# A four-layer vision block on one core: roots of the last layer norm in two chains instead of three, and half of a mask multiplication moved behind the transposes

## The chip, the cores and the metric

The kernel runs on one core of a Trainium2 chip. The metric is the device time of one execution in microseconds. The engines are PE (TensorE, matrix products and transposes), DVE (VectorE), ACT (ScalarE), POOL (GpSimd) and SP (SyncE, which here only issues DMAs). They run their own instruction streams and wait for each other through semaphores.

## The reference

The input is x, 128 x 128 positions with 32 channels. Four layers follow, each added to its input:

```python
x = x + L0_conv(ln_c(x), mask0, ...)
t = t + L0_ffn(ln_t(t), W, V, gamma, beta)       # a recurrence with a sigmoid
x = x + L1_conv(ln_c(x), mask1, ...)
t = t + L1_ffn(ln_t(t), router_w, router_b, expert_w, expert_b)   # 2 of 8 experts per token

def L1_conv(z, mask, ...):
    zn = layer_norm(z)
    a = mask * sigmoid(zn @ w_ag + b_ag) * (zn @ w_ap + b_ap)
    b = mask * sigmoid(zn @ w_bg + b_bg) * (zn @ w_bp + b_bp)
    p = einsum('bikc,bjkc->bijc', a, b)          # for each channel a 128x128x128 product
    return (layer_norm(p) @ w_z + b_z) * sigmoid(zn @ w_g + b_g)
```

The change concerns the third layer (its masks) and the layer norm ahead of the fourth (its roots).

## The kernel before

The 128 rows lie on the 128 partitions. Each partition holds 128 tokens of 32 channels. Work is cut into 8 groups of 16 tokens (GROUPS), and sums for the layer norms into 4 quarters of 32 tokens (QUARTERS). Nothing plans the order at run time: each engine's instructions are written out in one list, and an engine executes them strictly in that order. "Waits" below are waits on a semaphore at the head of such a list.

**Layer norms.** A `Norm` object has pieces, ranges of tokens for which the roots are taken together. For each quarter DVE makes the sums (`take_sum`, L331) and the sums of squares (`take_squares`, L369) of squares that ACT (`take_square`, L337) or POOL (L346) has made. `take_var` then runs a chain of eleven small DVE instructions (L375 to L398), each waiting for the one before; the last raises `done`. The length of an instruction of the chain hardly depends on how many tokens the piece has.

**Third layer, input stage.** `n_c` has pieces of 32, 32 and 64 tokens. For each group POOL (`scale_c`, L361, two instructions) multiplies by the roots (DVE does it for groups 0 and 1), PE transposes (`turn_group`, L651), ACT copies to SBUF (`copy_c`, L1607), PE makes the logits of the output gate (L1326) and, in two halves, the projections (L1338, biases by L1158). PE's order is that of `groups_held`: head 0, head 1, tail 0, head 2, tail 1, head 3, tail 2, tail 3, head 4, head 5, tail 4, and so on, a head being the transposes and a tail the projections. ACT takes the sigmoids (`gates_c`, L1613 and L1620), DVE multiplies both (`gate_c`, L1941) into `gated`, which is laid out [token i, channel, token j] with 64 channels (32 of a, then 32 of b). PE's half h of tail g waits until DVE has done the gate of the same half of group g - 1, which frees the PSUM banks. POOL multiplies `gated` by the mask, two instructions per group (`mask_half`, L833, all 64 channels). `mask_e` is the mask in the order of `gated`, built from `mask_c` before the stage. PE has twelve idle products (L1133) after the last tail and then waits for all sixteen masks.

**Third layer, products.** For q = 0 to 7, PE transposes 4 channels of a into bank q % 2 (L1362) and 4 of b into bank 2 + q % 2 (L1364). ACT copies the first to `gated_t` (L1638), DVE the second (L1972), PE multiplies them (L1353), ACT keeps the product (L1627) and squares it (L1633), DVE makes the partial sums (L1963, L1968). POOL has the bias of the gated output meanwhile (L941, L946). After it, DVE takes the roots, multiplies PE's projections by the gates (L1994) and POOL adds them to `x2` (L872).

**Fourth layer, input stage.** `n_d` has pieces of 32, 32 and 64 tokens. DVE takes the roots of quarter 0 as soon as its squares are summed, those of quarter 1 after its own, and those of quarters 2 and 3 together. POOL's `scale_d` waits for the roots of a piece and then scales its groups (L626, one instruction each). PE transposes them (L651) and makes the router's logits (L1417), ACT copies the transposed groups (`copy_d`, L1660). ACT's list is: squares of quarters 0, 1 and 2, `copy_d` of groups 0 and 1, square of quarter 3, `copy_d` of groups 2 and 3, and so on. From group 1's copy on, SP issues DMAs that repeat the transposed x in `out_gate` and, from group 3's copy on, in `x` (`copy_x`, L731). DVE chooses the two experts of each token in quarters 0 and 1 (`choose`, L2040 to L2066); after that PE spreads the weights (L1447), DVE weighs x by them (L2074), PE multiplies with the experts (L1468), ACT keeps the sum (L1697) and PE turns it back (L1479), group by group.

Of the kernel before, what the change touches and what calls it, by code (L numbers as in the profile page):

```python
# [35 lines left out]
P = 128  # L36
C = 32
# [37 lines left out]
def build(nc, a, out):  # L75
    ctx = ExitStack()
    with ctx:
        def sb(name, shape, dt=F32):
            return ctx.enter_context(nc.sbuf_tensor(name, shape, dt))

        def sem(name):
            return ctx.enter_context(nc.semaphore(name))
# [49 lines left out]
        mid128 = sb("mid128", [P, P])  # L132
        x2 = sb("x2", [P, P, C])
        mask_e = sb("mask_e", [P, P])
        ident_b = sb("ident_b", [P, P], BF16)
        pick = sb("pick", [P, S, 2, P], BF16)
        eighth = sb("eighth", [P, 16])
# [80 lines left out]
        a_copied = sem("a_copied")  # L218
        rows_built = sem("rows_built")
        w_scaled = sem("w_scaled")  # L220
        w_repeated = sem("w_repeated")
        w_kept = sem("w_kept")
        o_built = sem("o_built")
# [128 lines left out]
        def scale_c(eng, q, st, signal, early=False):  # L352

            g = 2 * q + st
            if not early:
                eng.wait_ge(p_c.turned, g - 1)
            src = in_parts(x2, st, q)
            r = in_order(rstd, st, q)
            for h in range(2):
                dst = xn[:, st, 2 * h:2 * h + 2, :].rearrange("p t (r s c) -> p r t s c", r=2, c=C)  # L360
                ins = eng.tensor_tensor(dst, src[:, 2 * h:2 * h + 2, :, :]  # L361
                                        .rearrange("p r (t s) c -> p r t s c", t=2),
                                        r[:, 2 * h:2 * h + 2, :].unsqueeze(3).to_broadcast([P, 2, GROUP, C])
                                        .rearrange("p r (t s) c -> p r t s c", t=2), ALU.mult)
            ins.then_inc(signal, 1)
# [146 lines left out]
        n_b = Norm("nb", C, 1.0, EPS_LN, ((0, P),), 3)  # L512
        n_c = Norm("nc", C, pieces=((0, 32), (32, 64), (64, 128)), **both)
        n_z = Norm("nz", C, 1.0, EPS_LN, ((0, P),))
        n_d = Norm("nd", C, 1.0, EPS_LN, ((0, 32), (32, 64), (64, 128)))

        def x_q(q):
            return x[:, q * QT:(q + 1) * QT, :]
# [257 lines left out]
        def _(pool):  # L776
# [45 lines left out]
            def mask_gated(pj, msk, chans, per):  # L822

                def f(g, s, early):
                    n = 16 // per
                    if msk is mask_a:
                        pool.wait_ge(ld_m, 16)
                    for h in range(per):
                        pool.wait_ge(pj.used, per * g + h + 1)
                        m = msk[:, :].rearrange("p (g k) -> p g k", k=n)[:, bass.ds(per * g + h, 1), :]  # L830
                        v = gated[:, 0:chans, :].rearrange("p o (g k) -> p g o k", k=n)
                        v = v[:, bass.ds(per * g + h, 1), :, :].rearrange("p a o k -> p (a o) k")
                        pool.tensor_tensor(v, v, m.to_broadcast([P, chans, n]), ALU.mult).then_inc(pj.masked, 1)  # L833
                return f
# [88 lines left out]
            for q in range(2):  # L923
                pool.wait_ge(y_added, q + 1)
                square_c(pool, q).then_inc(n_c.squared, 1)
            mask_half = mask_gated(p_c, mask_e, 2 * C, 2)
            for g in (2, 3):
                pool.wait_ge(n_c.done, 2)
                scale_c(pool, g // 2, g % 2, p_c.scaled)
            mask_half(0, 0, False)  # L930
            pool.wait_ge(n_c.done, 3)
            for g in range(1, GROUPS):
                if g + 3 < GROUPS:
                    scale_c(pool, (g + 3) // 2, (g + 3) % 2, p_c.scaled)
                mask_half(g, g % 2, False)

            def gate_bias(g):
# [175 lines left out]
        def _(pe):  # L1113
# [227 lines left out]
                    ins.then_inc(halves, 1)  # L1341

            groups_held(pe, turn_group(pe, p_c), project_c)
            idle_products(0, 12)
            pe.wait_ge(p_c.masked, 2 * GROUPS)
            def c_products(q):
                b = bank(4 + q % 2)
# [162 lines left out]
        def _(act):  # L1510
# [110 lines left out]
                                   ACT.Sigmoid).then_inc(p_c.gates, 1)  # L1621

            groups_held_copies(act, copy_c, gates_c, begun=lambda: square_late(3))

            def keep(q):
                act.wait_ge(f_prod, q + 1)
# [115 lines left out]
        def _(dve):  # L1742
# [210 lines left out]
            sum_c(dve, 3)  # L1953
            gate_c(1, 1)
            chain(dve, late_squares(3))
            dve.wait_ge(p_c.masked, 2)
            take_var(dve, n_c, 2)
            with dve.Fori(2, GROUPS) as g:
                for h in range(2):
                    gate_c(g, h)  # L1960
            def part_sum(n):
                dve.wait_ge(f_kept, 2 * n + 2)
                return dve.tensor_reduce(sg[:, 0, P * n:P * n + P], prod_t[:, :, 8 * n:8 * n + 8], AX.X, ALU.add)  # L1963
# [5 lines left out]

            for q in range(8):  # L1970
                dve.wait_ge(f_turn, q + 1)
                dve.tensor_copy(gated_t[:, C + 4 * q:C + 4 * q + 4, :].rearrange("p a b -> p (a b)"),  # L1972
                                bank(2 + q % 2)).then_inc(f_copy_v, 1)
                if q in (2, 4, 6):
                    part_sum(q // 2 - 1)
                if q in (3, 5, 7):
                    part_squares(q // 2 - 1)
# [25 lines left out]
            for m in range(4):  # L2003
# [3 lines left out]
                gate_z(2 * m + 1)  # L2007
                if m == 2:
                    take_sum(dve, n_d, x2, 0, z_added)
            chain(dve, take_squares(dve, n_d, 0))  # L2010
            take_var(dve, n_d, 0)


            for q in range(1, QUARTERS):
                take_sum(dve, n_d, x2, q, z_added)
                chain(dve, take_squares(dve, n_d, q))
                if q != 2:
                    take_var(dve, n_d, min(q, 2))

            def choose(q, n):  # L2020

# [111 lines left out]
```

## Time and profile before

| | us |
|---|---|
| median of 3 runs | 304.37 (304.34 to 304.86) |
| the profiled execution | 304.54 |
| its span, first to last instruction | 302.8 |
| PE, DVE, POOL, ACT busy | 232.0, 225.8, 158.5, 117.3 |
| of that between 136 and 178.5 us (length 42.50) | 36.92, 28.96, 26.83, 20.88 |
| between 178.5 and 203 us (24.50) | 22.48, 19.53, 19.94, 16.45 |
| between 218 and 233 us (15.00) | 8.83, 13.87, 4.59, 3.45 |
| between 233 and 247 us (14.00) | 13.01, 13.11, 5.82, 5.48 |

Times in the profile count from the span's start. The chain of waits follows the work that ended last back through whatever released it; a timeline lists the instructions of one engine, merging neighbours of one kind, with the idle time before them and who ended it in brackets. PEclk is the granted clock of PE as a share of 2.4 GHz.

### The profile page before, as it was taken

The numbers are of one execution on the slowest core, as the hardware profiler recorded it, in microseconds if no ns is written. First come the engines' busy times: TensorE is split into PE (matmuls) and PEld (weight loads), VectorE is DVE, ScalarE is ACT, GpSimd is POOL, SyncE is SP. The second block draws the span as 40 slices with busy tenths as digits, with TensorE's granted clock in tenths as the row PEclk, the third lists the DMA queues.
The fourth block names the chain that finished last, engine by engine and source line by source line (L and its number), as shares of the span: only waits on it lengthen the run. The fifth ranks groups of instructions, "written<-read, shape, count | busy, mean of one in ns | idle before, by whom it ended". The sixth has DMA issues, their size and how long they took to land.

```text
span 302.8 us, 4655 instructions
## 1 busy us (share of the span) xinstructions
PE 232.0 (77%) x1578; PEld 163.3 (54%) x1578; DVE 225.8 (75%) x395; ACT 117.3 (39%) x226; POOL 158.5 (52%) x223
## 2 busy tenths in 40 slices
PE   0286896666399799998969999793156999889894
PEld 0175782344144489985747769692146962333331
DVE  4999638978877500687974547899899997898893
ACT  4353533335223155555535538742221341221210
POOL 4444880379400188221559989927842438875100
PEclk9999997969589999999999999999555555999998
DMA  6200000000000000000000000000018952869201
GB/s 221 71 15 4 0 2 0 0 1 2 0 0 0 0 0 3 0 2 2 1 0 2 0 1 2 2 0 1 0 35 202 207 114 62 182 182 203 103 35 69
DMA packets 6635, 13.08 MB, mean 43 GB/s; under 512 B 2774, under 2 KB 3030, under 8 KB 6614
## 3 DMA queue, kind: packets, MB, share of 16 engines
q1 hardware_dynamic: 6470, 12.81, 16.6%
q8 instruction: 12, 0.20, 0.3%
q14 instruction: 9, 0.07, 0.1%
q10 hardware_dynamic: 144, 0.01, 0.0%
HBM read 2.32 MB, written 2.10 MB: 15 GB/s over the span
## 4 chain that ended last, share of the span: by engine, by line
PE 44%; DVE 34%; issue 6%; POOL 6%; ACT 6%; DMA 2%; SPq 1%; DVEq 0%; POOLq 0%; ACTq 0%
PE ps L1468 5%; PE ps L1061 4%; PE ps L1057 4%; DVE var L369 4%; PE ps L1133 3%; PE ps L1447 3%; DVE sums L331 3%; POOL x L872 3%; PE ps L1353 2%; PE ps L1338 2%; PE ps L651 2%; DVE gated L1941 2%; PE ps L1460 2%; POOL gated L833 2%; PE ps L1244 2%
## 5 line engine op out<-in xcount | busy, mean ns | idle before, releaser
L651 PE MATMUL ps<-ident,xn 128*128 128x128 f32 x144 | 29.1, 337 | 21.3 <-DVE xn L641 10.1
L651 PEld LDWEIGHTS ps<-ident,xn 128*128 128x128 f32 x144 | 19.9, 173 | 33.9 <-issue 8.8
L872 POOL TENSOR_TENSOR x<-x,sg 128x512 f32 x16 | 22.0, 1392 | 9.1 <-DVE sg L1994 7.6
L1133 PE MATMUL ps<-ones_b,ones_h 128*128 128x512 bf16 x55 | 17.4, 470 | 10.2 <-ACT v_wrap L1569 7.2
L1941 DVE TENSOR_TENSOR gated<-ps,sg 128x512 f32 (+1 forms) x16 | 16.5, 1043 | 10.8 <-ACT sg L1620 10.5
L1094 ACT ACTIVATE gated_t<-ps,bn 128x128 f32<-128x128 f32 x54 | 16.9, 364 | 13.8 <-PE ps L1061 12.9
L833 POOL TENSOR_TENSOR gated<-gated,mask_e 128x512 f32<-128x512 f32 x16 | 20.0, 1278 | 2.1 <-DVE gated L1941 2.1
L660 ACT ACTIVATE xt<-ps 128x512 f32<-128x512 f32 (+1 forms) x24 | 12.3, 525 | 22.0 <-PE ps L651 17.2
L1447 PE MATMUL ps<-gated,pick 96*128 96x512 bf16 x64 | 20.3, 428 | 0.1
L369 DVE TENSOR_REDUCE var<-squares 128x32 f32<-128x1024 f32 (+1 forms) x18 | 19.6, 1090 | 0.8 <-POOL squares L346 0.8
L337 ACT ACTIVATE squares<-x 128x1024 f32<-128x1024 f32 x12 | 12.7, 1056 | 14.2 <-POOL x L872 11.2
L1158 PE MATMUL ps<-rows,ones_b 64*128 64x512 bf16 x64 | 13.2, 407 | 6.1 <-issue 2.8
L331 DVE TENSOR_REDUCE sums<-x 128x32 f32<-128x1024 f32 x12 | 14.5, 1211 | 4.1 <-DMA x<-in_x_dram 2.8
L1061 PE MATMUL ps<-gated_t,v_t 128*128 128x128 f32 (+1 forms) x104 | 17.3, 289 | 0.0
L752 POOL CAST b_hi<-b_full 128x64 bf16<-128x64 f32 (+1 forms) x3 | 0.8, 272 | 30.6 <-DVE w_bs L1860 25.4
L1057 PE MATMUL ps<-gated,w_bs 128*128 128x128 f32 (+1 forms) x104 | 16.3, 280 | 0.6 <-DVE w_bs L1860 0.4
L1338 PE MATMUL ps<-w_c,xt 64*128 64x256 f32 x128 | 16.4, 376 | 0.0
L1133 PEld LDWEIGHTS ps<-ones_b,ones_h 128*128 128x128 bf16 x55 | 6.0, 117 | 18.4 <-issue 8.4
L1697 ACT ACTIVATE xt<-ps 128x512 f32<-128x512 f32 x8 | 4.8, 597 | 28.7 <-PE ps L1468 28.7
L361 POOL TENSOR_TENSOR xn<-x,rstd 128x256 f32<-128x256 f32 x12 | 7.1, 622 | 16.7 <-DVE rstd L398 16.7
L833 POOL TENSOR_TENSOR gated<-gated,mask_a x8 | 11.5, 1464 | 7.8 <-DVE rstd L398 6.4
L879 POOL TENSOR_TENSOR sg<-sg,mask_a 128x512 f32<-128x512 f32 x8 | 8.4, 1049 | 13.4 <-DVE sg L1804 13.4
(279 smaller groups left out, 635.8 us busy)
## 6 DMA issues: line engine op xcount, KB each, us to landing
out_gate<-gated SPq DMA_DIRECT2D x32, 128.0 KB, 2.3
x<-gated SPq DMA_DIRECT2D x32, 128.0 KB, 2.3
x<-in_x_dram SPq DMA_DIRECT2D x4, 512.0 KB, 5.6
out_dram<-x SPq DMA_DIRECT2D x8, 256.0 KB, 2.0
e_full<-in_L_ffn_expert_b_dram SPq DMA_DIRECT2D x12, 1.0 KB
mask_a<-in_L_conv_mask_dram SPq DMA_DIRECT2D x1, 64.0 KB, 6.1
mask_c<-in_L_conv_mask_dram SPq DMA_DIRECT2D x1, 64.0 KB, 1.8
w_x<-in_L_ffn_expert_w_dram SPq DMA_DIRECT2D x1, 32.0 KB
```

Source lines behind the costliest of these rows:

```text
L331: ins = dve.tensor_reduce(quarter(sums, q), quarter(src, q), AX.X, ALU.add)
L369: return dve.tensor_reduce(quarter(var, q), quarter_of(squares, q, nm.chans), AX.X, ALU.add)
L651: ins = pe.transpose(bank(s)[:, t * P:(t + 1) * P], xn[:, s, t, :], ident[:, :])
L833: pool.tensor_tensor(v, v, m.to_broadcast([P, chans, n]), ALU.mult).then_inc(pj.masked, 1)
L872: pool.tensor_tensor(v, v, sg[:, s, :], ALU.add).then_inc(pj.added, 1)
L1057: pe.matmul(summed(st, k, b), w_bs[:, :], flat(x_cm, CHUNK * st + k), start=True, stop=False, skip_group_check=True)
L1061: pe.matmul(summed(st, k, b), v_t[:, :], flat(y_cm, CHUNK * st + k - 1), start=False, stop=True, skip_group_check=True).then_inc(stepped[s ...
L1094: act.activation(flat(y_cm, k + CHUNK * st), bank(2 + 2 * st + b)[:, 0:P], ACT.Sigmoid, bias=bn[:, 9:10]).then_inc(state[st], 1)
L1133: pe.matmul(bank(b).rearrange("p (k o) -> p k o", o=P), ones_h[:, :], ones_b[:, :].unsqueeze(1).to_broadcast([P, GROUP, P]), start=True, s ...
L1338: ins = pe.matmul(d, xt[rs, s, 2 * h + t, :], w_c[rs, :, 2 * r:2 * r + 2, :].rearrange("p h s c -> p h (s c)"), start=False, stop=(t == 1) ...
L1447: ins = pe.matmul(bank(PAIRS[u % 3] + h), pick[0:K3, s, h, :], w_t[:, GROUP * P * G:GROUP * P * (G + 1)], start=True, stop=True, skip_grou ...
L1941: dve.tensor_tensor(o, v, sg[:, h, :].rearrange("p (u s o) -> p u s o", u=2, s=S), ALU.mult).then_inc(p_c.used, 1)
```

## The change

Third layer. DVE makes gate (2,0) before the third root chain and gate (2,1) after it. POOL masks only the 32 channels of a (`mask_gated(p_c, mask_e, C, 2)`), and scales one group further ahead of its masks. PE transposes the mask into bank 6 after the last tail and has ten idle products in place of twelve; ACT copies it to `mask_t`; DVE's eight copies of the transposed b become products with `mask_t`.

Fourth layer. `n_d` gets the default pieces, 64 and 64 tokens. DVE takes the roots after quarters 1 and 3.

```diff
-        n_d = Norm("nd", C, 1.0, EPS_LN, ((0, 32), (32, 64), (64, 128)))
+        n_d = Norm("nd", C, 1.0, EPS_LN)
@@ POOL
-            mask_half = mask_gated(p_c, mask_e, 2 * C, 2)
+            mask_half = mask_gated(p_c, mask_e, C, 2)
...
             pool.wait_ge(n_c.done, 3)
+            scale_c(pool, 2, 0, p_c.scaled)
             for g in range(1, GROUPS):
-                if g + 3 < GROUPS:
-                    scale_c(pool, (g + 3) // 2, (g + 3) % 2, p_c.scaled)
+                if g + 4 < GROUPS:
+                    scale_c(pool, (g + 4) // 2, g % 2, p_c.scaled)
                 mask_half(g, g % 2, False)
@@ PE
-            idle_products(0, 12)
+            pe.wait_ge(gate_kept, GROUPS - 1)
+            pe.wait_ge(p_c.masked, 1)
+            pe.transpose(bank(6)[:, 0:P], mask_e[:, :], ident[:, :]).then_inc(mask_turned, 1)
+            idle_products(0, 10)
@@ ACT
             groups_held_copies(act, copy_c, gates_c, begun=lambda: square_late(3))
+            act.wait_ge(mask_turned, 1)
+            act.activation(mask_t[:, :], bank(6)[:, 0:P], ACT.Copy).then_inc(mask_kept, 1)
@@ DVE
             chain(dve, late_squares(3))
+            gate_c(2, 0)
             dve.wait_ge(p_c.masked, 2)
             take_var(dve, n_c, 2)
-            with dve.Fori(2, GROUPS) as g:
+            gate_c(2, 1)
+            with dve.Fori(3, GROUPS) as g:
                 for h in range(2):
                     gate_c(g, h)
+            dve.wait_ge(mask_kept, 1)
...
-                dve.tensor_copy(gated_t[:, C + 4 * q:C + 4 * q + 4, :].rearrange("p a b -> p (a b)"),
-                                bank(2 + q % 2)).then_inc(f_copy_v, 1)
+                dve.tensor_tensor(gated_t[:, C + 4 * q:C + 4 * q + 4, :],
+                                  bank(2 + q % 2).rearrange("p (a b) -> p a b", b=P),
+                                  mask_t[:, :].unsqueeze(1).to_broadcast([P, 4, P]), ALU.mult).then_inc(f_copy_v, 1)
...
-            chain(dve, take_squares(dve, n_d, 0))
-            take_var(dve, n_d, 0)
+            take_squares(dve, n_d, 0)
             for q in range(1, QUARTERS):
                 take_sum(dve, n_d, x2, q, z_added)
                 chain(dve, take_squares(dve, n_d, q))
-                if q != 2:
-                    take_var(dve, n_d, min(q, 2))
+                if q % 2:
+                    take_var(dve, n_d, q // 2)
```

## Rows read from the trace of the kernel before

**Rows 1.** The page's fourth part: shares of the chain of waits by engine.
```profile
PE 44%; DVE 34%; issue 6%; POOL 6%; ACT 6%; DMA 2%; SPq 1%; DVEq 0%; POOLq 0%; ACTq 0%
```

**Rows 2.** Chain of waits, 136 to 236 us: start, length, what.
```profile
154.84 1.19 POOL xn L361 x2
156.03 2.46 POOL gated L833 x2
158.50 1.16 POOL xn L361 x2
...
178.48 0.66 PE ps L1362 x4
```

**Rows 3.** Timeline of DVE, 134 to 200 us.
```profile
152.00 0.23 DVE L375 SCALAR_TENSOR_TENSOR newton<-sums 128x64 f32<-128x64 f32 x1
...
154.86 1.91 DVE L1941 TENSOR_TENSOR gated<-ps,sg 128x512 f32 x2
...
174.83 2.12 DVE L1941 TENSOR_TENSOR gated<-ps,sg 128x512 f32 x2 [1.35 <-ACT sg L1620]
179.61 0.69 DVE L1972 COPY gated_t<-ps 128x512 f32<-128x512 f32 x1 [2.66 <-PE ps L1364]
```

**Rows 4.** Timeline of PE, 136 to 202 us.
```profile
155.94 0.39 PE L1158 MATMUL ps<-rows,ones_b 64*128 64x512 bf16 x2 [2.49 <-DVE gated L1941]
...
157.03 0.38 PE L1158 MATMUL ps<-rows,ones_b 64*128 64x512 bf16 x2
...
158.21 0.66 PE L651 MATMUL ps<-ident,xn 128*128 128x128 f32 x4
...
160.19 0.38 PE L1143 MATMUL ps<-rows,ones_h 128*128 128x512 bf16 x1
...
175.05 2.76 PE L1133 MATMUL ps<-ones_b,ones_h 128*128 128x512 bf16 x12
```

**Rows 5.** Timeline of ACT, 136 to 202 us: the copy of group 4.
```profile
158.90 0.60 ACT L1607 ACTIVATE xt<-ps 128x512 f32<-128x512 f32 x1
```

**Rows 6.** The instructions of line 1994: shortest, median and longest in ns, first and last start.
```profile
L1994 DVE TENSOR_TENSOR sg<-ps,out_gate x8: 678/681/691, 205.4 to 215.7; 128x512 f32<-128x512 f32 x8
```

**Rows 7.** Timeline of DVE, 198 to 256 us.
```profile
216.35 1.21 DVE L369 TENSOR_REDUCE var<-squares 128x32 f32<-128x1024 f32 x1
217.59 0.83 DVE L375 SCALAR_TENSOR_TENSOR newton<-sums 128x32 f32<-128x32 f32 x1
...
227.67 1.22 DVE L331 TENSOR_REDUCE sums<-x 128x32 f32<-128x1024 f32 x1
228.81 1.21 DVE L369 TENSOR_REDUCE var<-squares 128x32 f32<-128x1024 f32 x1
230.05 0.22 DVE L375 SCALAR_TENSOR_TENSOR newton<-sums 128x64 f32<-128x64 f32 x1
...
247.91 2.34 DVE L2074 TENSOR_TENSOR prod<-ps,out_gate 128x1024 f32<-128x1024 f32 x2
```

**Rows 8.** Timeline of POOL, 198 to 256 us: scaling of groups 0 and 1.
```profile
220.74 2.06 POOL L626 TENSOR_TENSOR xn<-x,rstd 128x512 f32<-128x512 f32 x2 [2.37 <-DVE rstd L398]
```

**Rows 9.** Timeline of ACT, 202 to 256 us: the square of quarter 3.
```profile
224.50 1.05 ACT L337 ACTIVATE squares<-x 128x1024 f32<-128x1024 f32 x1
```

**Rows 10.** Timeline of PE, 202 to 256 us: transposes of groups 4 and 5.
```profile
234.00 1.12 PE L651 MATMUL ps<-ident,xn 128*128 128x128 f32 x4 [2.32 <-POOL xn L626]
...
236.47 1.09 PE L651 MATMUL ps<-ident,xn 128*128 128x128 f32 x4
```

**Rows 11.** Timeline of SP, 218 to 262 us: the first block of copied x.
```profile
224.62 10.39 SPq L731 DMA_DIRECT2D out_gate<-gated  x16
```

**Rows 12.** Windows of 2 us: length, busy PE, PEld, DVE, ACT, POOL; PEclk, DMA.
```profile
256.00:258.00 2.00, 1.85 (x11) 0.63 (x8) 0.62 (x1) 0.83 (x3) 1.83 (x4) 0.80 0.93 211
```

**Rows 13.** Chain of waits, 232 to 303 us: expert products of groups 0 and 1.
```profile
253.20 3.62 PE ps L1468 x16
...
261.90 1.90 PE ps L1468 x16
```

More of the change, by code:

```diff
@@ L134, in build @@
         mask_e = sb("mask_e", [P, P])
+        mask_t = sb("mask_t", [P, P])
         ident_b = sb("ident_b", [P, P], BF16)
@@ L220, in build @@
         w_scaled = sem("w_scaled")
+        mask_turned = sem("mask_turned")
+        mask_kept = sem("mask_kept")
         w_repeated = sem("w_repeated")
```

## The prediction

> **What bounds the kernel now.** I read the chain of waits first. Over the whole span it is mostly PE and DVE [rows 1], so a gain has to come from places where PE waits for another engine. In the second convolution's input stage (136 to 178.5 us) the reader is to see the chain leave PE twice. At 154.84 POOL scales group 4, then masks two halves for 2.46, and only then scales group 5, whose transposes start on PE at 159.70, right behind that scaling [rows 2]. At the end POOL masks the last half after DVE's last gate, and PE takes up the transposes at 178.48 [rows 2]. The timeline of DVE shows why the first hole begins: the eleven small root instructions run from 152.00, and gate (2,0) stands behind them at 154.86 [rows 3], while PE has been idle for 2.49 when it takes up group 3's first half at 155.94 [rows 4]. Between the two holes PE is continuous, so what is won at 160 is still there at 175.
>
> In the experts' input stage (216 to 248 us) the chain is DVE: reductions, roots, reductions, roots, reductions, roots, then the choice of experts. PE idles until POOL scales, and POOL until the roots are done [rows 7, 8]. After 248 us PE, ACT and DVE hand on to each other in a fixed rhythm, which I take to shift as a whole.
>
> **Part 1, masks and order in the convolution.** The numbers are times of the profiled execution, and I follow each engine through.
>
> - gate_c(2,0) now goes ahead of the roots. It starts at 152.00 and takes 0.95 (half of 1.91) [rows 3]; the roots move to 152.95 and take the same 2.84 (152.00 to POOL's start at 154.84) [rows 2, 3], so n_c.done comes just before 155.79. Gate (2,1) runs then, to 156.83.
> - PE does group 3's first half without a wait, but its second half needs gate (2,1): it starts at about 156.87 in place of 157.03 [rows 4]. The stall of 2.49 does not go: it moves behind the first half, and only 0.16 is won. Group 4's transposes follow at 158.21 - 0.16 = 158.05 [rows 4].
> - POOL scales groups 4 and 5 back to back from 155.79, 1.19 each [rows 2]: both are done at 158.17, where group 5 was done at 159.66 before (158.50 + 1.16). PE takes group 5 right behind group 4, at 158.5. So POOL's hole of 1.2 at 159.70 is gone, and the next to be late is ACT: its copy of group 4 starts 1.87 after PE's second half does (158.90 - 157.03) [rows 4, 5] and takes 0.60, so it ends at 159.34, and group 4's projections start at 159.38, where they started at 160.19 [rows 4]. Won: 0.81. From here on PE has its old rhythm, and POOL, with masks half as long, is ahead of it.
> - The masks: sixteen of 128x512 become sixteen of 128x256. 1.23 to 1.27 each becomes about 0.62 (half of 1.23; POOL's scalings of 128x256 take 0.60) [rows 2]; bounds 0.60 and 0.75. Only the last lies on the path. DVE's last gate ends at 176.95 (174.83 + 2.12) [rows 3], 0.81 earlier after the change: 176.14. Then 0.07 of handing on, the mask of 0.65, 0.04: PE can start at 176.90 in place of 178.48. The last mask used to wait out the one before it, too; that one now ends in time. Won here: 1.58 - 0.81 = 0.77.
> - PE's filling work has to end by then. Twelve idle products take 2.76 [rows 4], 0.23 each; ten are 2.3, and the new transpose of the mask some 0.2 to 0.3 with its two waits, both on things long done. 174.24 + 0.3 + 2.3 = 176.84 against 176.90: it just fits; a miss would cost 0.1 to 0.3. ACT's copy of the turned mask lies in its idle time between 175 and 178; covered by that idle time it costs nothing, without the cover its own 0.3 to 0.4.
> - The masks of the second half now ride on DVE: eight PSUM copies of 0.69 [rows 3] become eight products of PSUM with SBUF, written in contiguous rows. The trace has that kind twice. The gate of the last stage, PSUM by SBUF to contiguous rows, takes 0.68 [rows 6]; gate_c, whose writes go down a stride of 128 elements, takes 1.06 (2.12 / 2) [rows 3]. Nearest is the first, in operands and in its writes: I take plus 0.00 each. With 1.06 it would be up to 8 x 0.37 = 3.0.
>
> So part 1 gives -1.58 (bounds: -0.8 if the first hole stays, +1.4 if each masked copy takes 1.06 and nothing covers it).
>
> **Part 2, two root chains in place of three.** All times here would be 1.58 earlier; I leave the shift out and add it at the end.
>
> - One chain of eleven goes, and its waiting. The first one began with an instruction of 0.83 at 217.59, where the same kind at 230.05 takes 0.22 [rows 7]. That was beside POOL's last additions. The Trainium skill (GPSIMD Engine Reference, "Specifications") says that POOL's SBUF interface is shared with VectorE, with contention for VectorE instructions with two SBUF inputs; this row agrees, 0.83 against 0.22. By it the new masked copy, with one input in PSUM, is not held up, and the sum stays as it is.
> - DVE after: squares of quarter 0 at 216.35, sums of quarter 1 and its squares each 1.13 on (227.67 to 228.81 is such a step), then 1.24 until a waiting successor (228.81 to 230.05) [rows 7]: 216.35 + 1.13 + 1.13 + 1.24 = 219.85. Roots over 64 columns take 2.84: POOL's scaling starts at 222.69, in place of 220.74 [rows 8]. So the first two groups get later by 1.95.
> - That delay has a taker that the diff does not show. ACT has the square of quarter 3 in its queue behind the copies of groups 0 and 1, which wait for PE's transposes of just these groups. It ran at 224.50 for 1.05, so it was ready 4.81 after POOL's start (225.55 - 220.74) [rows 8, 9]. After: 222.69 + 4.81 = 227.50. DVE would be there for it at 222.5 + 1.13 + 1.24 + 1.13 = 226.0 and waits 1.5. Its reduction starts at 227.55 in place of 228.81 [rows 7], and everything behind, the second roots and the choice, is 1.26 earlier, not 2.8.
> - PE is in time for that: at half clock a transposed and routed group takes 2.47 (234.00 to 236.47) [rows 10]. From 223.8, one transpose (0.9) and three such groups end at 232.1; group 4 is scaled for 234.00 - 1.26 = 232.74. Logits of quarter 0 come at about 230, before 231.5 when DVE asks.
> - The copies of the normalised x start with group 1's, now 1.95 later. Sixteen take 10.39 [rows 11]: 226.6 to 237.0, and DVE's weighing reads them from 247.91 - 1.26 [rows 7]. Ten microseconds of cover: no cost.
>
> Part 2 gives -1.26 (bounds: -2.8 with no wait for the square; 0 if the second chain is held up as much as one chain is worth).
>
> **Sum.** -0.81 - 0.77 - 1.26 = -2.84. The profiled execution took 304.54 (span 302.8 and 1.74 around it): 301.7. The median of the runs is 0.17 below the profiled one, which is within what I leave open, so **301.7**.
>
> **The rivals.**
>
> - *The clock of PE comes back at another moment.* The granted clock is at 0.5 (1.2 of 2.4 GHz) from 213 to 256.7, through transposes and routing products that keep PE busy, and is whole from 257 on [rows 12]. The sixteen expert products of a group take 3.62 at half and 1.90 at full clock [rows 13], so each group more at half costs at least 1.72 and each one less gives it back. The sum above takes the return to move with the work. If the whole first group runs at full clock: 301.7 - 1.7 = 300.0, or a little less with the spreading products. If two groups more run at half: 301.7 + 3.4 = **305.1, slower**; it decides from about 1.6 groups on. For it: the work before it gets denser by parts and may look different to the chip. Against: from 234 on the sequence on PE is the same, only earlier. The Trainium skill (TensorE: Matmul & The Clock Gate, "What's actually happening") says that the moment of the return depends on where the work falls against something that runs free of the kernel's start; by it either side is possible after a shift of 2.8, and one case here cannot show it.
> - *The masked copy is as slow as gate_c* (1.06). DVE in the products' stage has little idle time after its third copy, so about 2.0 of the 3.0 come through: 303.7. Against it: [rows 6].
> - *The first hole stays* (gate (2,1) or the copy of group 4 later than I have it): 0.8 less, 302.5.
> - *Nobody waits for the square of quarter 3*: 1.5 more, 300.2. It needs ACT to get there without the first groups; its order on ACT is written out, so I hold it unlikely.
> - That the change does nothing (POOL off the path anyway) is against [rows 2], where POOL has the chain at both holes: 304.4.
>
> **Numbers.** Forecast 301.7: 0.54. Early clock 300.0: 0.12. Late clock 305.1: 0.05. Slow masked copy 303.7: 0.09. First hole stays 302.5: 0.10. No wait for the square 300.2: 0.07. Nothing 304.4: 0.03. A measurement of this kernel can tell about 0.2% (0.6 us) from no change. Faster than 303.76 are all but the late clock, the nothing and half of the slow copy: 0.87; within 0.2%: 0.08; slower: 0.05. The range for 8 in 10 takes in the early clock and the slow copy: 299.7 to 303.8.
>
> **What would show it.** After the change: gate (2,0) ahead of the roots and PE's wait between the halves of group 3, about 2.1 long; projections of group 4 right behind ACT's copy; POOL's masks near 0.63; masked copies of 0.69 on DVE; a DVE wait of about 1.5 for ACT's square ahead of the last reduction of squares, with the second roots about 2.8 earlier than before in all; transposes after the idle products 1.6 earlier. The forecast is wrong if the masked copies are well over 0.7, if the square of quarter 3 is there before DVE asks, or if the expert groups' first run at another clock than before.

## The result and the profile after

| | before | after |
|---|---|---|
| median, 18 runs each, taken together | 305.05 (304.34 to 307.56) | 303.43 (301.52 to 306.77) |
| ratio, 95% interval | | 0.9932 (0.9914 to 0.9951) |
| profiled execution | 304.54 | 301.52 |
| its span | 302.8 | 299.7 |

The change makes the kernel faster by 0.68%, 2.1 us. (The ratio leaves out disturbed runs and weighs the kernels in the same rounds; the plain medians differ by 1.6.) The prediction said 301.7 from 304.4, 0.9% or 2.8 us; the profiled execution has 3.0 less, but it is the fastest of its 18. By the interval the gain is 1.5 to 2.6, and the forecast lies just above that. Of the 1.7 by which the median, 303.43, lies above 301.7, 0.7 is in the kernel before, whose median of 18 is 305.05 and not 304.37. So two questions stand: are the steps of the sum there, and where does the better part of a microsecond stay in the other executions?

The profiled execution first. Its line numbers are a little higher (L1941 is now L1950, L369 is L372, L651 is L654, L833 is L836). The unchanged part of the kernel, up to the end of the recurrence, took 0.68 longer than in the execution before: DVE's first comparison of the end states starts at 136.16, before at 135.48. All comparisons below take this 0.68 off. The timeline of DVE in the convolution (start, length, engine, line, what):

```profile
136.16 0.29 DVE L1902 TENSOR_TENSOR dif<-gated_t,ends 128x128 f32<-128x128 f32 x1 [0.89 <-ACT gated_t L1098]
...
152.69 1.05 DVE L1950 TENSOR_TENSOR gated<-ps,sg 128x512 f32<-128x512 f32 x1
153.58 0.21 DVE L378 SCALAR_TENSOR_TENSOR newton<-sums 128x64 f32<-128x64 f32 x1
...
156.25 1.91 DVE L1950 TENSOR_TENSOR gated<-ps,sg 128x512 f32<-128x512 f32 x2
...
178.67 1.50 DVE L1984 TENSOR_TENSOR gated_t<-ps,mask_t 128x512 f32<-128x512 f32 x2 [2.06 <-PE ps L1371]
181.55 0.69 DVE L1984 TENSOR_TENSOR gated_t<-ps,mask_t 128x512 f32<-128x512 f32 x1 [1.38 <-PE ps L1371]
```

The reader sees gate (2,0) ahead of the roots, and the masked copy at the 0.69 of the plain one [rows 3]. PE's timeline of the same stretch:

```profile
157.33 0.39 PE L1162 MATMUL ps<-rows,ones_b 64*128 64x512 bf16 x2 [2.00 <-DVE gated L1950]
...
158.51 1.09 PE L654 MATMUL ps<-ident,xn 128*128 128x128 f32 x8
159.86 0.39 PE L1147 MATMUL ps<-rows,ones_h 128*128 128x512 bf16 x1 [0.25 <-ACT xt L1614]
...
174.89 2.32 PE L1137 MATMUL ps<-ones_b,ones_h 128*128 128x512 bf16 x10
177.47 0.66 PE L1369 MATMUL ps<-ident,gated 128*128 128x128 f32 x4 [0.26 <-POOL gated L836]
```

The wait of 2.49 [rows 4] is one of 2.00, in the middle of group 3 (about 2.1 was expected). Groups 4 and 5 are transposed in one go, and group 4's projections wait 0.25 for ACT's copy. POOL's timeline has the two scalings together and the shorter masks:

```profile
156.41 2.34 POOL L364 TENSOR_TENSOR xn<-x,rstd 128x256 f32<-128x256 f32 x4 [7.97 <-DVE rstd L401]
158.71 1.41 POOL L836 TENSOR_TENSOR gated<-gated,mask_e 128x256 f32<-128x256 f32 x2
...
176.70 0.72 POOL L836 TENSOR_TENSOR gated<-gated,mask_e 128x256 f32<-128x256 f32 x1 [0.34 <-DVE gated L1950]
```

The experts' input stage on DVE:

```profile
215.39 1.21 DVE L372 TENSOR_REDUCE var<-squares 128x32 f32<-128x1024 f32 x1
...
218.89 0.23 DVE L378 SCALAR_TENSOR_TENSOR newton<-sums 128x64 f32<-128x64 f32 x1
...
223.94 1.22 DVE L334 TENSOR_REDUCE sums<-x 128x32 f32<-128x1024 f32 x1
226.57 1.22 DVE L372 TENSOR_REDUCE var<-squares 128x32 f32<-128x1024 f32 x1 [1.41 <-ACT squares L340]
227.82 0.23 DVE L378 SCALAR_TENSOR_TENSOR newton<-sums 128x64 f32<-128x64 f32 x1
...
245.68 2.35 DVE L2086 TENSOR_TENSOR prod<-ps,out_gate 128x1024 f32<-128x1024 f32 x2
```

There is the foretold wait for ACT's square of quarter 3, 1.41 (1.5 was expected), and ACT's timeline has that square where it was expected, behind the copy of group 1:

```profile
225.00 0.60 ACT L1669 ACTIVATE gated<-ps 128x512 f32<-128x512 f32 x1 [0.41 <-PE ps L654]
225.49 1.05 ACT L340 ACTIVATE squares<-x 128x1024 f32<-128x1024 f32 x1
```

The last difference is PE's clock. Here are a window of 1 us (its columns are those of [rows 12]) and the chain's row of the first expert group, at 0.5 of the clock for a part and at 1.00 for the rest; before, the return fell into 256 to 258 [rows 12] and the sixteen products took 3.62 [rows 13]:

```profile
252.00:253.00 1.00, 1.00 (x8) 0.13 (x4) 0.89 (x1) 0.00 (x0) 0.92 (x2) 0.69 0.00 0
```
```profile
250.97 2.74 PE ps L1475 x16
```

The balance of the two profiled spans: +0.68 in the unchanged part, -2.91 up to the weighing (245.68 - 0.68 = 245.00, against 247.91), -0.87 behind it, nearly all of it these sixteen products (3.62 - 2.74). Together -3.10, which is 299.7 - 302.8.

### The profile page after: what moved, and what is told of

Read it like the earlier page. It is cut to its first block, busy times and chain, and to the rows that moved or that the text cites. A ratio compares the mean times of both kernels' runs of the same rounds, so it can differ in the third digit from the quotient of the medians.

```text
span 299.7 us, 4638 instructions
## 1 busy us (share of the span) xinstructions
PE 232.7 (78%) x1577; PEld 164.8 (55%) x1577; DVE 223.3 (74%) x384; ACT 117.5 (39%) x227; POOL 150.2 (50%) x223
## 4 chain that ended last, share of the span: by engine, by line
PE 43%; DVE 37%; issue 6%; ACT 6%; POOL 5%; DMA 2%; SPq 1%; DVEq 0%; POOLq 0%; ACTq 0%
PE ps L1475 5%; PE ps L1065 4%; PE ps L1061 4%; DVE var L372 4%; DVE sums L334 4%; PE ps L1454 3%; PE ps L654 3%; POOL x L875 3%; PE ps L1342 3%; PE ps L1360 2%; DVE gated L1950 2%; PE ps L1467 2%; PE ps L1248 2%; DMA raw<-in_L_conv_gi_b_dram 2%; DVE squares L2086 2%
## 5 line engine op out<-in xcount | busy, mean ns | idle before, releaser
L654 PE MATMUL ps<-ident,xn 128*128 128x128 f32 x144 | 29.7, 343 | 18.3 <-DVE xn L644 9.0
L654 PEld LDWEIGHTS ps<-ident,xn 128*128 128x128 f32 x144 | 20.5, 177 | 30.7 <-issue 10.3
L1137 PE MATMUL ps<-ones_b,ones_h 128*128 128x512 bf16 x53 | 16.5, 464 | 10.4 <-ACT v_wrap L1576 7.5
L1950 DVE TENSOR_TENSOR gated<-ps,sg 128x512 f32 (+1 forms) x16 | 16.6, 1048 | 10.0 <-ACT sg L1627 9.8
L372 DVE TENSOR_REDUCE var<-squares 128x32 f32<-128x1024 f32 (+1 forms) x18 | 19.6, 1091 | 2.2 <-ACT squares L340 1.4
L836 POOL TENSOR_TENSOR gated<-gated,mask_a x8 | 11.5, 1468 | 8.0 <-DVE rstd L401 6.5
L836 POOL TENSOR_TENSOR gated<-gated,mask_e 128x256 f32<-128x256 f32 x16 | 11.5, 738 | 7.5 <-DVE gated L1950 7.5
```

Of the source, the lines that this page charges most:

```text
L372: return dve.tensor_reduce(quarter(var, q), quarter_of(squares, q, nm.chans), AX.X, ALU.add)
L654: ins = pe.transpose(bank(s)[:, t * P:(t + 1) * P], xn[:, s, t, :], ident[:, :])
L1137: pe.matmul(bank(b).rearrange("p (k o) -> p k o", o=P), ones_h[:, :], ones_b[:, :].unsqueeze(1).to_broadcast([P, GROUP, P]), start=True, s ...
L1950: dve.tensor_tensor(o, v, sg[:, h, :].rearrange("p (u s o) -> p u s o", u=2, s=S), ALU.mult).then_inc(p_c.used, 1)
```

## The experiments

Twelve kernels ran beside the kernel before. Their profiled executions differ in the unchanged part (it ends between 135.06 and 137.75), so I compare stretches between instructions: **S1** from DVE's first comparison of end states (L1902) to PE's first transpose of the products (L1369); **S2** from the first to the last reduction of squares in the last layer norm (L372); **S3** from the last of these to the first weighing (L2086); **S4** from there to the span's end (good to 0.05, as the page gives the span to 0.1). "Fall" says whether PE's granted clock leaves 1.00 anywhere from 136 to 206 us.

| kernel | S1 | fall | S2 | S3 | S4 | ratio to before (95%) |
|---|---|---|---|---|---|---|
| before | 43.00 | no | 12.46 | 19.10 | 54.89 | |
| after | 41.31 | no | 11.18 | 19.11 | 54.02 | 0.9932 (0.9914 to 0.9951) |
| after, once more | 42.51 | yes | 11.17 | 19.09 | 54.09 | 0.9929 (0.9905 to 0.9953) |
| masks alone | 42.54 | yes | 12.45 | 19.10 | 54.00 | 0.9977 (0.9951 to 1.0004) |
| roots alone | 43.02 | no | 11.18 | 19.09 | 53.99 | 0.9935 (0.9913 to 0.9958) |
| square first | 42.56 | yes | 9.67 | 19.62 | 53.85 | 0.9897 (0.9862 to 0.9931) |
| gate back | 41.51 | no | 11.18 | 19.11 | 54.53 | 0.9908 (0.9875 to 0.9940) |
| order only | 43.27 | yes | 11.17 | 19.11 | 53.91 | 0.9924 (0.9888 to 0.9960) |
| hole filled | 41.33 | no | 11.17 | 19.10 | 54.01 | 0.9866 (0.9816 to 0.9916) |
| hole filled, POOL's old order | 42.11 | no | 11.18 | 19.11 | 54.31 | 0.9884 (0.9852 to 0.9916) |
| warm | 42.51 | yes | 10.72 | 19.11 | 54.25 | 0.9922 (0.9886 to 0.9959) |
| all | 41.32 | no | 9.69 | 21.87 | 55.37 | 0.9887 (0.9843 to 0.9931) |
| hole filled, square first | 41.33 | no | 9.68 | 19.62 | 53.88 | 0.9872 (0.9827 to 0.9917) |
| gate back, square first | 41.51 | no | 9.68 | 19.61 | 55.09 | 0.9856 (0.9822 to 0.9889) |

Between the end of S1 and the start of S2 all fourteen take 37.87 to 37.97. In time, the roots alone (0.9935) are as fast as the whole change (0.9932), and the masks alone are not clear of no change: what the masks and the order add to the roots is not visible in these ratios, only in S1.

**Masks alone.** The changed kernel, with the three pieces of the last norm and DVE's lines for them as before (the diff shows the first line only).

```diff
-        n_d = Norm("nd", C, 1.0, EPS_LN)
+        n_d = Norm("nd", C, 1.0, EPS_LN, ((0, 32), (32, 64), (64, 128)))
```

> Part 1 alone (masks and order of the convolution; roots of the last norm in three chains as before). My theory, the sum of the prediction: from the last instruction of the unchanged recurrence to PE's first transpose of the products (178.48 before) 1.6 to 1.7 us less, everything behind it unchanged in its steps, so about 1.6 less than before in time (ratio 0.9945 to 0.995). The rival, that the parts only pay together (because the shift itself moves the return of PE's clock), has the landmark 1.6 earlier but less than 0.8 of it in the time.

Neither theory had this right: S1 is only 0.46 shorter. Every instruction stands in the order of the changed kernel, but PE's transposes of groups 4 and 5 take 1.97 in place of 1.09, and the windows of 1 us (length; busy PE, PEld, DVE, ACT, POOL; PEclk) show why:

```profile
158.67 0.39 PE L1162 MATMUL ps<-rows,ones_b 64*128 64x512 bf16 x2 [2.01 <-DVE gated L1950]
159.86 1.97 PE L654 MATMUL ps<-ident,xn 128*128 128x128 f32 x8
```
```profile
158.00:159.00 1.00, 0.33 (x4) 0.31 (x6) 1.00 (x2) 0.00 (x0) 1.00 (x3) 1.00 0.00 0
159.00:160.00 1.00, 1.00 (x11) 0.62 (x8) 0.50 (x1) 0.03 (x1) 1.00 (x2) 0.92 0.00 0
160.00:161.00 1.00, 1.00 (x6) 1.00 (x7) 0.29 (x1) 0.57 (x1) 1.00 (x3) 0.50 0.00 0
161.00:162.00 1.00, 1.00 (x5) 0.74 (x4) 0.76 (x1) 0.74 (x2) 1.00 (x2) 0.50 0.00 0
162.00:163.00 1.00, 1.00 (x6) 0.94 (x5) 0.00 (x0) 0.46 (x1) 1.00 (x3) 0.50 0.08 16
163.00:164.00 1.00, 1.00 (x9) 0.85 (x10) 0.00 (x0) 0.28 (x1) 1.00 (x3) 0.88 0.00 0
```

PE's clock falls to 1.2 GHz for 3.4 us. The fall begins 1.2 after the end of the wait of 2.01 that the moved gate left. S1 is 42.54 - 41.31 = 1.23 longer than in the changed kernel's profiled execution, which has no fall.

**Roots alone.** The kernel before with the two-piece norm and its DVE lines (the diff shows the first line only); nothing of part 1.

```diff
-        n_d = Norm("nd", C, 1.0, EPS_LN, ((0, 32), (32, 64), (64, 128)))
+        n_d = Norm("nd", C, 1.0, EPS_LN)
```

> Part 2 alone (roots of the last norm in two chains, convolution as before). My theory: DVE waits 1.4 to 1.5 for ACT's square of quarter 3, and the last reduction of squares starts 1.25 earlier relative to the first one than before, so about 1.25 less (ratio 0.996). The rival, that the later start of the first groups costs elsewhere as much as the saved chain, has the reduction 1.25 earlier and the weighing not, ratio 0.999 to 1.002.

S2 is 1.28 shorter and S3 unchanged, as my theory has it. The time fell by more, 0.65% or 2.0 us, and the forecast of 0.4% lies just below the interval (0.42% to 0.87%). In the profile the rest stands in S4, 0.90 shorter than before.

**Square first.** On the changed kernel:

```diff
             take_square(act, n_d, x2, 2, z_summed)
+            take_square(act, n_d, x2, 3, z_summed)
             copy_d(0, 0, True)
             copy_d(1, 1, True)
-            take_square(act, n_d, x2, 3, z_summed)
```

> The changed kernel with ACT's square of quarter 3 put ahead of its copies of groups 0 and 1. My theory, that DVE's 1.41 of waiting comes from ACT's order alone: the wait goes, the last squares' reduction starts 1.4 to 1.5 earlier after the first; PE is still busy with groups 2 and 3 and their routing until 232 in the old count and so takes group 4 only 0.4 to 0.5 earlier than in the changed kernel, while DVE's choice starts when the logits of quarter 0 are there. So 0.4 to 1.4 less than the changed kernel. The rival, that PE at half clock is the bound here: 0.5 at most.

S2 is 1.51 shorter: DVE's wait came from ACT's order alone. S3 is 0.51 longer, since now PE, at half clock, is behind. So 1.0 is left, inside the theory's bounds and beyond the rival's 0.5. ACT has the square ready at 218.7 now:

```profile
217.60 1.06 ACT L340 ACTIVATE squares<-x 128x1024 f32<-128x1024 f32 x1 [1.70 <-POOL x L875]
224.14 0.60 ACT L1669 ACTIVATE gated<-ps 128x512 f32<-128x512 f32 x1 [5.48 <-PE ps L654]
```

S1 has the fall again (42.56).

**Gate back.** On the changed kernel:

```diff
-            gate_c(2, 0)
             dve.wait_ge(p_c.masked, 2)
             take_var(dve, n_c, 2)
+            gate_c(2, 0)
             gate_c(2, 1)
```

> The changed kernel with gate (2,0) back behind the roots on DVE (its other edits stay). My theory: the roots come 0.9 earlier, PE waits for gate (2,0) ahead of the first half of group 3 and then runs both halves without a wait. The second half starts where it did before the change, so this edit was worth only 0.1 to 0.3 of part 1, and 0.8 of 0.81 was POOL's order. The rival, that the gate's place is what opened PE's hole: 0.7 or more slower than the changed kernel.

S1 is 41.51: without a fall the moved gate is worth 0.20, as expected. PE waits 2.30 ahead of group 3's first half and the clock stays whole. The ratio is lower than the changed kernel's, not higher. That is the direction to be expected if a fall costs 1.2 and the moved gate gives 0.20, but the intervals overlap, so the time alone does not show it.

**Hole filled.** On the changed kernel, in the projections:

```diff
                 for h in range(2):
+                    if g == 3 and h == 1:
+                        idle_products(0, 8)
                     if not (early and s == 0):
```

> The changed kernel with eight idle products on PE between the two halves of group 3, in the wait of 2.0 that the moved gate left there. In two of the four kernels run before that had this wait (masks alone, square first) the profiled execution shows PE at 1.2 GHz for 3.5 to 4 us from about there, and from the recurrence's end to the products' transposes 42.5 in place of 41.3; the kernel with the gate back in its old place has no such fall. My theory, that the reshaped hole lets the clock fall in part of the executions: here it stays at 2.4 GHz, the stretch is 41.3, and the median is 0.3 to 0.8 less than the changed kernel's against the same before (ratio about 0.991). The rival, that the falls are chance and have nothing to do with the hole: falls in as many executions, ratio 0.993 as the changed kernel's.

PE's timeline: the eight products fit (the wait left is 0.18), S1 is that of the changed kernel's execution without a fall, and the clock reads 1.00 throughout.

```profile
156.65 1.90 PE L1137 MATMUL ps<-ones_b,ones_h 128*128 128x512 bf16 x8
158.74 0.39 PE L1162 MATMUL ps<-rows,ones_b 64*128 64x512 bf16 x2 [0.18 <-DVE gated L1952]
159.92 1.09 PE L654 MATMUL ps<-ident,xn 128*128 128x128 f32 x8
```

The ratio, 0.9866 (0.9816 to 0.9916), is even lower than hoped for, with six runs and a wide interval. It is 2.0 us below the changed kernel's, more than the 1.2 that a fall costs, and the two intervals barely overlap: it agrees with the account, but its size is not explained by it.

**Warm.** On the changed kernel, to see what the clock costs ahead of the last layer's groups:

```diff
+            idle_products(1, 32)
             pe.wait_ge(e_built, 1)
             pe.wait_ge(p_z.used, GROUPS)
...
+            idle_products(1, 20)
             for g in range(GROUPS):
                 turn(g, g % 2, g < 2)
```

> The changed kernel with idle products on PE where it waits ahead of the last layer: 32 behind the last projections of the gated output and 20 ahead of the first transposes. It tests what the half clock from 211 to 253 costs. If the clock stays at 2.4 GHz into the groups 0 to 3, their transposes take 0.66 in place of 1.1, ACT's square of quarter 3 comes 0.8 to 1.0 earlier, and so do the second roots and the choice: 0.8 to 1 less than the changed kernel; if it lasts into the first expert group too, another 1 to 2.5 less. The rival, that PE's clock costs nothing there because DVE is the bound: under 0.3.

Half of it came: groups 0 and 1 are transposed at full clock and S2 is 0.46 shorter. Then the clock falls, at 228.0. The idle products end before POOL has scaled, and PE waits 2.12 ahead of group 0 and 0.35 ahead of group 1:

```profile
225.56 0.66 PE L654 MATMUL ps<-ident,xn 128*128 128x128 f32 x4 [2.12 <-POOL xn L629]
226.57 0.66 PE L654 MATMUL ps<-ident,xn 128*128 128x128 f32 x4 [0.35 <-POOL xn L629]
```

The windows of 2 us:

```profile
226.00:228.00 2.00, 1.65 (x15) 1.43 (x14) 1.86 (x2) 1.33 (x3) 2.00 (x3) 1.00 0.00 0
228.00:230.00 2.00, 2.00 (x12) 2.00 (x11) 1.16 (x1) 1.41 (x2) 0.53 (x1) 0.50 0.44 98
230.00:232.00 2.00, 2.00 (x11) 2.00 (x12) 1.73 (x9) 0.63 (x2) 0.00 (x0) 0.50 0.90 207
```

It returned at 255.3, although from 234.04 on PE had no wait. So it came back no earlier for the expert groups, S4 is not shorter, and the ratio is that of the changed kernel.

**Order only.** On the changed kernel:

```diff
-            mask_half = mask_gated(p_c, mask_e, C, 2)
+            mask_half = mask_gated(p_c, mask_e, 2 * C, 2)
...
-                dve.tensor_tensor(gated_t[:, C + 4 * q:C + 4 * q + 4, :], ... mask_t ..., ALU.mult)
+                dve.tensor_copy(gated_t[:, C + 4 * q:C + 4 * q + 4, :].rearrange("p a b -> p (a b)"), bank(2 + q % 2))
```

> The changed kernel with the masks as before (POOL over all 64 channels, plain copies by DVE): only the orders of part 1 are left of it, with the transposed mask made but not used. My theory: the first hole's gain stays (0.8 without a fall of the clock) and the end's gain goes, since POOL's last mask takes 1.27 and waits out the one before it: transposes of the products 0.7 to 0.8 later than in the changed kernel, and DVE's copies take 0.69 as its products with the mask did. Ratio about 0.0025 higher than the changed kernel's. The rival, that the masked copy on DVE costs something that its duration does not show: less than 0.4 later.

S1 is 43.27 with a fall, against 42.51 to 42.56 in the four executions with a fall and the new masks: 0.71 to 0.76 longer, as my theory says, and DVE's first two plain copies take the same 1.50 as the masked ones:

```profile
178.47 2.50 POOL L836 TENSOR_TENSOR gated<-gated,mask_e 128x512 f32<-128x512 f32 x2 [0.97 <-DVE gated L1950]
```
```profile
182.22 1.50 DVE L1984 COPY gated_t<-ps 128x512 f32<-128x512 f32 x2 [2.77 <-PE ps L1371]
```
```profile
181.02 0.66 PE L1369 MATMUL ps<-ident,gated 128*128 128x128 f32 x4 [0.97 <-POOL gated L836]
```

The ratio does not show it; its interval is too wide for 0.0025.

**All.** Square first, hole filled, the warm kernel's idle products, and:

```diff
+                if g == 4:
+                    idle_products(5, 10)
                 turn(g, g % 2, g < 2)
...
                 spread_w(G, 1)
+                if G == 0:
+                    pe.wait_ge(chosen, STEPS + 2)
+                    idle_products(3, 14)
```

> A version meant to be faster than both: the changed kernel with the square of quarter 3 first, the filled hole at group 3, the idle products of the warm kernel, ten more ahead of group 4's transposes and fourteen ahead of the third spreading product of the expert stage. My theory: the square's wait goes (1.4), the clock stays up through the input stage of the experts and the first expert group takes 1.9 for its sixteen products in place of 2.7 to 3.6: 299 to 300 us, ratio 0.980 to 0.985. The rival, that the idle products land at half clock and stand in the way: 301 or more.

The rival holds. The idle products found the clock at half and stood in the way: ten took 4.45, fourteen 5.24, and DVE waited 2.26 for the spreading products behind the fourteen.

```profile
230.29 4.45 PE L1137 MATMUL ps<-ones_b,ones_h 128*128 128x512 bf16 x10
234.54 1.06 PE L654 MATMUL ps<-ident,xn 128*128 128x128 f32 x4
...
245.27 5.24 PE L1137 MATMUL ps<-ones_b,ones_h 128*128 128x512 bf16 x14
```

The sixteen products took 1.92, as hoped, but so they did with the square first and with the hole filled, where no idle products stand ahead of them. S3 and S4 are longer by 2.8 and 1.35 than in the changed kernel.

**Hole filled, square first.** The two edits that had worked, without the idle products of the last layer:

> The changed kernel with the filled hole at group 3 and ACT's square of quarter 3 first, without the idle products of the last layer, which earned nothing. My theory: the stretch to the products' transposes is 41.3 in every execution, the last squares' reduction comes 9.7 after the first (11.2 in the changed kernel), the choice of experts then waits 0.5 more ahead of the weighing since PE is behind. So 1.0 less than the changed kernel from the square and about half of 1.2 from the hole: ratio to before 0.984 to 0.988, faster than the changed kernel beside it by 0.4 to 0.6%.

S1 41.33 and S2 9.68, as expected. 301.24, ratio 0.9872 (0.9827 to 0.9917): faster than the kernel before, and 1.6 below the changed kernel's 302.85 in the same rounds, the forecast being 0.4 to 0.6%. Against the kernel with only the hole filled (0.9866) the square's 1.0 does not show in the ratio; both have six runs.

**After, once more.** No edit.

> The changed kernel once more, on the same chip as the others of this call. My theory, that the moved gate's hole lets PE's clock fall in part of the executions: a second profile may show the fall near group 3 (stretch 42.5) or not (41.3); the median is above e_best's by 0.4 to 0.6%, ratio to before 0.992 to 0.995. The rival, that part 1 has all its gain and the first 18 runs were unlucky: ratio 0.989 to 0.991, which is what the steps of the profile promise.

This profiled execution has the fall (S1 42.51), and the ratio repeats itself, 0.9929. The rival's 0.989 to 0.991 lies below the first interval (from 0.9914) and reaches only the lower end of this one (0.9905), so it is unlikely.

```profile
156.49 0.39 PE L1162 MATMUL ps<-rows,ones_b 64*128 64x512 bf16 x2 [2.00 <-DVE gated L1950]
157.69 1.97 PE L654 MATMUL ps<-ident,xn 128*128 128x128 f32 x8
```

**Hole filled, POOL's old order.**

```diff
-            scale_c(pool, 2, 0, p_c.scaled)
             for g in range(1, GROUPS):
-                if g + 4 < GROUPS:
-                    scale_c(pool, (g + 4) // 2, g % 2, p_c.scaled)
+                if g + 3 < GROUPS:
+                    scale_c(pool, (g + 3) // 2, (g + 3) % 2, p_c.scaled)
                 mask_half(g, g % 2, False)
```

> The changed kernel with the filled hole, and POOL's old order: scaling of group 5 behind the (now shorter) masks of group 1. It sizes POOL's part of the first hole. My theory: group 5 is scaled 1.4 later, PE's transposes of it likewise, and group 4's projections start behind them, 0.7 to 0.8 later than with the new order: stretch 42.0 to 42.1, ratio 0.0025 above that of the same kernel with the new order. The rival, that the shorter masks alone do it: stretch 41.3 to 41.5.

S1 is 42.11, 0.78 more than with the new order. PE waits for the scaling of group 5 again:

```profile
158.93 0.66 PE L654 MATMUL ps<-ident,xn 128*128 128x128 f32 x4
160.57 0.66 PE L654 MATMUL ps<-ident,xn 128*128 128x128 f32 x4 [0.98 <-POOL xn L364]
```

**Gate back, square first.** The edits of those two kernels together.

> The changed kernel with gate (2,0) back behind the roots and the square of quarter 3 first. My theory: no fall of the clock at group 3 (as in the other kernel with the gate in its old place), stretch 41.5, and the square's gain of 1.0: within 0.3 of e_best, so filling the hole and not making it are worth the same. The rival, that the clock falls here as often as with the moved gate: 0.3% or more slower than e_best.

S1 41.51, no fall, median 301.34, 0.1 from the kernel with the hole filled and the square first. The sixteen products of the first expert group take 3.62 here, as long as in the kernel before, and S4 is 55.09.

## Why the prediction was right, and what it did not see

**The first hole, forecast -0.81.** Group 4's projections start at 159.86 - 0.68 = 159.18, 1.01 earlier than at 160.19 [rows 4]. The extra 0.2 is mostly the handing on from the roots to gate (2,1), which starts 0.16 before POOL does (156.25 against 156.41). POOL's order gives 0.78 of it (42.11 against 41.33), the gate's place 0.20 (41.51 against 41.31).

**The end of the masks, forecast -0.77.** Measured 0.68: S1 is 1.69 shorter in all, and 1.01 was won before. A mask of 256 elements takes 0.72, not the 0.65 of the sum, and the idle products ended 0.26 ahead of it. Taking the masks' halving back cost 0.71 to 0.76 (order only).

**The masked copy at no cost.** 0.69 in the trace, like the plain copy. The rival of 1.06 per copy is out, and its reason with it: gate_c's longer time goes with its strided writes, or with something else in it that this product hasn't.

**Part 2, forecast -1.26.** Measured -1.28 (12.46 to 11.18), with the wait of 1.41 where it was placed. That ACT's order made the wait the square-first kernel shows: with the square ahead of the copies S2 is 9.67. The 0.83 of the first root instruction [rows 7] is gone as well: it now runs at 218.89, behind POOL's last addition, and takes 0.23. Nothing else in part 2 moved: the copies of x, PE's routing and DVE's choice were in time (S3 19.10 and 19.11).

**The sum.** -2.91 up to the weighing, against -2.84. In the time, 2.1 came. The agreement of the profile with the sum is in part luck: it needs an execution without the fall told of below, and this was the only one of six.

**What it did not see.** The prediction shifted the wait of 2.49 into the middle of group 3 and priced this at 0.16 won. It looked for PE's clock in the last layer and not here, where it read 1.00 all through the profile before. With the moved gate and nothing in the wait, five of six profiled executions show the clock at 1.2 GHz for about 3.4 us around group 4. In the four of these with the new masks S1 is 1.20 to 1.25 longer than in the sixth. The sixth, without the fall, is the first of the changed kernel, its fastest run. Of the eight other profiled executions (the kernel before, roots alone, both with the gate back, the four with the hole filled) none has the fall. Were the two kinds alike, so clean a split would come by chance about once in 330. The fill is the test that changes nothing but PE's idleness there: no fall in all four kernels that have it, and S1 of 41.3 in the three of them with POOL's new order.

Is that the missing part of the time? By an estimate with five in six, the fall costs 1.0 on average: 2.91 - 1.0 = 1.9, against 2.1 measured; for masks alone 1.69 - 1.0 = 0.7, against 0.7 measured (0.0023 x 304.56, interval 0 to 1.5). The numbers agree, but the balance is not closed. It leaves S4 out, which is 0.9 shorter than before in most kernels. If that belonged to the change, 1.9 would be 2.8. And the roots alone gained 2.0 in time (1.3 to 2.6), where S2 and S3 account for 1.3. So the fall and its 1.2 are shown in the profiles; that it is what the median lacks is likely and not shown.

What stays open: why a wait of 2.0 between the halves lets the clock fall, and one of 2.3 to 2.5 ahead of both does not. The form of the wait is not the only difference. Counted from the first comparison of end states it opens at 18.0 in the four kernels with the old gate and at 19.2 in the six with the moved one. The execution without the fall has the same wait as the five with it, so the form alone does not decide. What differs there is the clock's own history. PE's clock had last returned to 1.00 at 85.4, and the wait opens 70.0 after that. In the five with a fall it opens 68.4 to 69.4 after the last return, in the four with the old gate 67.3 to 67.6 after it. So the moment may count, and not what stands on either side. No kernel here has the old wait at another moment, so this stays untested. I also can't read the falls from unprofiled runs, so five in six is a count of profiles, not of runs.

The Trainium skill (TensorE: Matmul & The Clock Gate, "What's actually happening") stood behind the rival on the return of the clock in the last layer. The return did move: 3.62 became 2.74 for the sixteen products, while S4 of kernels with the same last layer lies between 53.99 (roots alone) and 54.53 (gate back). That agrees with its saying that the moment is not tied to the kernel's start. The prediction named another clock in the first expert group as a sign of being wrong, and this sign came: the sum had nothing for it, and the profiled execution won 0.87 there, half of what the rival of the early clock gave a whole group. Over the twelve kernels of the experiments the sixteen products take from 1.92 (square first, hole filled) to 3.62 (gate back, square first), so the one profile of the kernel before has one of the two longest. Whether the return moves with the change or from run to run, one profile per kernel does not show.

## What to carry to other kernels

Moving a wait is not free even if its length hardly changes: on PE look at the granted clock around its new place, in several executions, since one profile can be the lucky one. Here a wait in a dense stretch was filled with idle products for nothing, since they ended before it did; where the clock was at half already they took about twice their time (0.45 each in place of 0.23) and were in the way. And where a chain is merged, follow the first consumers: an engine whose written order puts shared work behind them hands the delay back.

## What the runs showed of the hardware

- PE's clock fell to 1.2 GHz behind a wait of 2.0 us in a stretch that was otherwise dense, in five of six profiled executions, and came back 3.4 us later; the price was 1.2 us.
- It can stay at 1.2 GHz while PE is busy: in the warm kernel from 228.0, behind waits of 2.12 and 0.35, until 255.3, the last 21 us of it without a wait (128-column float32 transposes, routing products of 32 columns and spreading products; windows busy 2.00 of 2.00).
- The unchanged first 136 us took 135.06 to 137.75 in fourteen profiled executions, with the clock's falls and returns at other places in most of them. A difference of 1 us between two profiles of this kernel says little unless both are measured from a common instruction.
- A VectorE product of PSUM with a broadcast SBUF operand, 128x512 in float32 with contiguous writes, takes 0.69, as long as a plain copy out of PSUM.
